# Eight dense products of 480 columns ahead of the channel loop of a three-stage attention kernel

## The reference, cut to what matters

```python
vf = v.reshape(b, l, NH * DV)
fir_short = causal_dwconv(vf, fir_short_w.reshape(NH * DV, FIR_S)).reshape(b, l, NH, DV)
fir_long = causal_dwconv(vf, fir_long_w.reshape(NH * DV, FIR_L)).reshape(b, l, NH, DV)
...
T = jnp.linalg.inv(jnp.eye(chunk, dtype=q.dtype) + A)
```

## Time and profile before

| | us |
|---|---|
| median of 3 runs | 3137.67 |
| the fastest and the slowest of them | 3137.32, 5492.04 |
| the profiled execution: its device time | 3131.47 |
| the profiled execution: its span, first to last instruction | 3129.7 |
| first stage, by the timeline | 0 to 929 |
| middle stage, by the timeline | 930 to 1158 |
| third stage with its setup, by the timeline | 1158 to 3130 |

### The profile page before, as it was taken

One profiled execution on the slowest core, in us unless ns is written; L12 is line 12 of the kernel. 1 busy time (PEld: TensorE's weight loads), 2 busy tenths in 40 slices (PEclk: granted clock), 3 DMA queues, 4 the chain that ended last, 5 costly groups with the idle time before them and its releaser, 6 DMA issues.

```text
span 3129.7 us, 54689 instructions
## 1 busy us (share of the span) xinstructions
PE 2781.5 (89%) x18016; PEld 2012.6 (64%) x18016; DVE 1992.9 (64%) x5332; ACT 1380.4 (44%) x2626; POOL 531.2 (17%) x375
## 2 busy tenths in 40 slices
PE   5999999999979945999999999999999999999997
PEld 3555555555548844767767676667767767767675
DVE  4777777777759923475665665665665665665664
ACT  3666665566642211344334344344334344334342
POOL 1222333222220000111111111111111111111110
PEclk9999999999975555799899899899989899899898
DMA  2555545455545762221211211211211221211200
GB/s 68 174 173 166 165 161 165 154 170 173 168 167 192 253 189 95 74 77 54 100 59 57 100 57 59 99 59 59 100 57 59 96 66 55 100 58 59 100 16 15
DMA packets 234755, 334.08 MB, mean 107 GB/s; under 512 B 115232, under 2 KB 200192, under 8 KB 225312
## 3 DMA queue, kind: packets, MB, share of 16 engines
q1 hardware_dynamic: 208704, 305.90, 29.8%
q10 hardware_dynamic: 24672, 12.58, 1.4%
q0 software_dynamic: 1152, 12.58, 1.0%
HBM read 191.68 MB, written 164.23 MB: 114 GB/s over the span
## 4 chain that ended last, share of the span: by engine, by line
PE 43%; DVE 10%; ACT 5%; issue 4%; DVEq 0%; ACTq 0%
PE bank L1403 6%; PE bank L1413 6%; PE bank L1346 5%; PE bank L1324 3%; PE bank L1357 3%; PE bank L1309 3%; PE bank L1375 3%; PE bank L1241 2%; PE bank L1350 2%; ACT L1550 2%; PE bank L1281 2%; PE bank L1273 2%; PE bank L1366 1%; DVE bst L1758 1%; PE bank L1317 1%
## 5 line engine op out<-in xcount | busy, mean ns | idle before, releaser
L680 DVE SCALAR_TENSOR_TENSOR Y<-bank,convw,Y 128x383 f32<-128x383 f32 (+2 forms) x576 | 315.6, 608 | 39.7 <-ACT Y L557 39.7
L1403 PE MATMUL bank<-YT,w1e 128*128 128x384 f32 x768 | 331.5, 560 | 1.7 <-ACT HE L1550 1.3
L1413 PE MATMUL bank<-w2e,HE 128*128 128x256 f32 x1152 | 319.4, 418 | 12.3 <-DVE HA L1822 9.4
L1822 DVE SCALAR_TENSOR_TENSOR HA<-bank,we,HA 128x256 f32<-128x256 f32 x576 | 242.7, 477 | 107.6 <-PE bank L1413 105.6
L409 PE MATMUL bank<-pb,wqkv 128*128 128x384 f32 x768 | 286.7, 496 | 0.5 <-DVE Y L680 0.5
L1707 DVE TENSOR_TENSOR L<-bank,b2g 128x48 f32<-128x48 f32 x32 | 6.7, 208 | 412.6 <-PE bank L1357 412.6
L1413 PEld LDWEIGHTS bank<-w2e,HE 128*128 128x128 f32 x1152 | 225.7, 208 | 55.3 <-issue 16.7
L779 POOL TENSOR_TENSOR RR<-RS,minus_half 128x24 f32<-128x24 f32 x32 | 133.2, 4162 | 430.0 <-DVE RS L727 430.0
L1403 PEld LDWEIGHTS bank<-YT,w1e 128*128 128x128 f32 x768 | 155.0, 220 | 79.4 <-issue 34.4
L1346 PE MATMUL bank<-qb,w1g 128*128 128x384 f32 x512 | 201.8, 517 | 0.4 <-ACT GH L1542 0.4
L1241 PE MATMUL bank<-qa 64*128 64x256 f32 x768 | 120.2, 435 | 91.2 <-PEq L1119 58.0
(11 more groups left out here) (220 smaller groups left out, 5786.1 us busy)
## 6 DMA issues: line engine op xcount, KB each, us to landing
packa<-pa SPq DMA_DIRECT2D x32, 1932.0 KB, 6.1
qa<-packa SPq DMA_DIRECT2D x32, 1932.0 KB, 7.9
packb<-pb SPq DMA_DIRECT2D x32, 768.0 KB, 3.5
qb<-packb SPq DMA_DIRECT2D x32, 768.0 KB, 6.3
toeplitz<-taps SPq DMA_DIRECT2D x128, 190.0 KB, 4.3
toep<-toeplitz SPq DMA_DIRECT2D x32, 760.0 KB, 4.3
packb<-fsk SPq DMA_DIRECT2D x32, 384.0 KB, 4.2
fl<-fl SPq DMA_DIRECT2D x32, 384.0 KB, 5.2
```

What stands on the lines that cost most here:

```text
L680: dve.scalar_tensor_tensor(out=Y[:, j, lag:T], in0=proj_bank[j][:, 0:T - lag], scalar=convw[:, j, CK - 1 - lag:CK - lag], in1=Y[:, j, lag: ...
L1403: mm = pe.matmul(bank[6][:, 0:T], w1e[:, a, k, :], YT[s][:, a, :], start=(a == 0), stop=(a == HALF - 1))
L1413: mm = pe.matmul(expert_bank(b), HE[k % 2][:, b * P:(b + 1) * P], w2e[:, k, :], start=True, stop=True)
L1822: dve.scalar_tensor_tensor(out=HA[s][:, b, :], in0=expert_bank(b), scalar=we[s][:, b, k:k + 1], in1=HA[s][:, b, :], op0=ALU.mult, op1=ALU. ...
```

## The change

Ahead of its loop over the channels PE issues eight matrix products with `ident` as the stationary matrix. Product k reads five channels of `v_all`, 5k to 5k+4, which is 480 moving columns, and writes them into `bank[4 + k % 4]`. Nobody reads these banks in the stage. The products wait for nothing and signal nothing. `ident` is taken out of `shared` for them. Nothing else is changed.

```diff
-    NB, NSYS, dram, bank, expanded = (shared[k] for k in ("NB", "NSYS", "dram", "bank", "expanded"))
+    NB, NSYS, dram, bank, expanded, ident = (shared[k] for k in ("NB", "NSYS", "dram", "bank", "expanded", "ident"))
...
             @block.tensor
             def _(pe):
+                def warm_up(n):
+                    for k in range(n):
+                        pe.matmul(bank[4 + k % 4][:, 0:5 * BLK * NB], ident[:, :],
+                                  v_all[:, 5 * k:5 * k + 5, :].rearrange("p c n -> p (c n)"), start=True, stop=True)
+
+                warm_up(8)
                 with pe.Fori(0, D // CG // 2) as i:
```

## The result

The changed kernel took 3190.54 us (median of four runs, 3179.44 to 3194.65) against 3139.39: 1.016 times the time before, 95% interval 1.0125 to 1.0194. It is about 50 us slower. The ratio leaves out one execution of the kernel before, the slow one of 5492.04 us. The forecast was 3136.7, range 3107 to 3147.

A forecast was written before the change was run, and what follows sets the result against it. The prediction took PE's low-clock channel loop to bound the middle stage. Start 930.15 + 8.2 products + 2 x 3.3 iterations + 1.4 pause = 946.4 against 947.4: 1.0 us gained, 3137.7 - 1.0 = 3136.7 us, range 3107 to 3147.

The forecast's parts named there:

- What bounds the middle stage, and the slack of 39 us: Middle stage: PE's channel loop at the low clock sets its end; the solver leaves at most 39 us to gain.
- The price of the dense products: Start of middle stage: the added products take 8.2 us, 930.15 to 938.35, with the clock rising 3.3 us in.
- An iteration at the high clock: Channel loop, first two iterations: 3.3 us each at the high clock, against 5.99 us at the low one.
- The pause and the fall: Ahead of the third iteration PE pauses 1.4 to 1.5 us for the third load, and the clock falls for good.
- rival (A): Middle stage: clock survives the third load until the solver's exchange; 22 us plus 1.0 gained, 3114.7 us; chance 0.24.
- A gain of 1.0 us, carried unchanged to the end: Third iteration starts at 946.4 instead of 947.4, and this 1.0 us lasts to the kernel's end.
- everything after is the same loop: From the third iteration on: same loop as before with loads issued in time, so the 1.0 us gain stays.
- on PE alone: Start of middle stage: the change removes and moves nothing, adding only 8 products, 16 records, on PE.
- last sign of being wrong altogether: Third stage: a span, from first load to end, changed by more than 5 us would make the forecast wrong altogether.
- Rival (C): Middle stage: clock does not rise during the added products; loss of 7.8 us, 3145.4 us; chance 0.08.
- bound of 8.4 us: Added products: a clock rise over 8.4 us in, or none, makes the kernel slower if the later loop stays low.
- Rival (D): Third stage meets the clock's ups and downs differently: some 5 to 10 us either way, atop each case; chance 0.08.

The follow-up runs named there:

- e6_half_loads: Changed kernel plus four 16-column products behind the eight dense ones, Toeplitz matrices loaded in halves with own semaphores: 3069.90 us, 0.9812 of the kernel before.
- e3_dense_loop: Changed kernel with the eight dense products written as a loop of eight turns, all into bank 4: 3146.56 us, 1.0032 of the kernel before.
- e2_dense8_short4: Changed kernel with four more products of 16 columns behind the eight dense ones, 16 more instructions: 3090.45 us, 0.9843 of the kernel before.
- e5_dense_loop_short10: Changed kernel with the eight dense products as a loop, then ten products of 16 columns: 3093.69 us, 0.9868 of the kernel before.
- e1_short8: Changed kernel with its eight products cut to 16 moving columns, same number of instructions: 3186.33 us, 1.0157 of the kernel before.

## Why the prediction was wrong

**What bounds the middle stage, and the slack of 39 us: right.** e6_half_loads took 33.8 of the 39, and no run went beyond it.

**The price of the dense products: right.** Forecast 8.2 us, from 930.15 to 938.35; measured 930.32 to 938.38. The rise came between 933 and 934 (taken: 3.3 us in).

**An iteration at the high clock: right.** 3.3 forecast, 3.21 measured.

**The pause and the fall: the event right, the reason not borne out.** The third load was issued at 941.84 (forecast 941.85) and landed 4.6 us later, in the upper part of the forecast 4.1 to 4.7, so the pause was 1.71 us, and the clock fell behind it. But the prediction put the line between living and falling at a pause of about 1.4 us, from the pauses ahead of L1309, and the length of the pause does not draw it. In this loop the clock stayed up behind 1.23 us (e3_dense_loop), 1.48 (e2_dense8_short4) and 1.55 (e6_half_loads), and fell behind 1.27 (e2_dense8_short4) and 1.41 (e5_dense_loop_short10). That this step came out as forecast is partly luck. Where the clock lived, rival (A) came with 18.8 us in the middle stage (22 and 1.0 forecast) and with its fall at the solver's exchange. What does decide stays open.

**"A gain of 1.0 us, carried unchanged to the end": wrong at both words.** The third iteration started 0.69 us earlier, and by the end of the stage later waits for loads (3.34 and 1.80 us, where it had been 0.70, 2.43 and 0.60) had turned that into 0.3 later. That is small. The step that failed is the sentence behind it, "everything after is the same loop", and before that the first sentence of the part on the change: that it adds 16 records "on PE alone". It costed the instructions by their work and their timing, and not by their place. They also moved the code of everything behind them by 32 instructions, and the head of the third stage's loop of 1731 records a turn, which had sat 37 instructions ahead of a piece's end, came to sit five ahead of it. That cost 30.1 us of pauses and 27.5 us of slower matmuls, over fifty times the term that I had worked out. The prediction's own last sign of being wrong altogether, a third stage that changes by more than 5 us, came with 56.2. That the slower matmuls follow from the pauses is argued from the fall behind them in the timeline. The length of the pauses does not give their size: in e3_dense_loop some 8 us more of them stand beside 45 us of slower matmuls.

The pauses of 2 us ahead of L1241, 13 of them and 26.7 us, and the 141 fetched pieces were in the trace and on the page of the kernel before. I read the waits of the middle stage only, as that was where the edit stood. With them the question would have been asked: what does the change do to a loop that already waits for its own code?

**Rival (C)** did not come. Its bound of 8.4 us was also miscounted: with no fast iteration the third one starts at 930.15 + 6.4 + 0.16 + 12.0 = 948.7 even with the clock high from the start, later than 947.4, and with two fast ones the bound is 8.2. **Rival (D)** named the right stage with the wrong cause and a fifth of the size or less: 5 to 10 us. e1_short8 shows that the loss needs nothing of the middle stage's clock. What (D) says of the clock is half of the loss all the same: a pause for code of 2 us and more at the head is followed by a low clock, as the pauses ahead of L1309 are the earlier trace rows.

## What to carry to other kernels

Any edit of a long unrolled engine program moves all code behind it. In this kernel the place of one loop was worth from 1.9% slower to 1.2% faster, with next to no work added. Look at the fetched instruction packets on the page and at waits for "issue" at loop heads before costing an edit by its work; and separate the two by a control that adds the same number of instructions without the work. Here ten idle products gained 1.2% where the eight dense ones alone lost 1.6%; the dense ones paid, by 30 us, once the code lay well and the loads went out earlier.

## What the runs showed of the hardware

- PE's loop is fetched anew in each turn, nine pieces of 16.4 KB (141 packets in the execution), or not at all (24 or 25); four added instructions decide (36: 3197.30 us, 40: 3101.04 us).
- A closing branch takes 3.4 to 4.2 us to the next instruction in the kernels that fetch in each turn, and 0.27 us in those that do not.
- A clock lifted by dense products of 480 columns can stay up over products that by themselves had run at 0.50 for 200 us: it was 1.00 from 938 to 991 in e3_dense_loop. It came back over these products, without dense ones, shortly after a fall: from 951 in e5_dense_loop_short10, from 997 in e6_half_loads.
- The length of a pause alone does not tell whether the clock falls. In the middle stage it stayed up behind 1.23, 1.48 and 1.55 us and fell in or right behind pauses of 1.27, 1.41, 1.71, 2.83, 2.98 and 3.00 us; ahead of L1309 it fell behind all twenty pauses of 1.42 or 1.43 us and stayed up behind 1.34.
